# Graph attention stage on one core: four of a step's 14 incidence matrices built by VectorE in one op, and own-edge messages signalled tile by tile

## The chip, the cores and the metric

The kernel runs on one NeuronCore of a Trainium2 chip. Its engines are TensorE (PE, matrix products into PSUM), VectorE (DVE), ScalarE (ACT), GpSimd (POOL) and SyncE (SP, which issues transfers here). They run side by side and meet at semaphores: an instruction raises one when it is done, and another engine's queue stands until a semaphore has reached a number. Within an engine the instructions keep the order of the program. The metric is the device time of one execution, in microseconds (us).

## What is computed

The reference is a stack of four graph layers on 50000 nodes with 64 features and 50000 edges. Each layer normalises the nodes, passes messages along the edges and adds the result to its input. The change lies in the third, a graph attention layer with 4 heads, of which this is the part that matters:

```python
src = jnp.concatenate([src0, jnp.arange(n, dtype=src0.dtype)])
dst = jnp.concatenate([dst0, jnp.arange(n, dtype=dst0.dtype)])
...
amax = jax.ops.segment_max(alpha, dst, num_segments=n)
ex = jnp.exp(alpha - amax[dst])
denom = jax.ops.segment_sum(ex, dst, num_segments=n)
alpha = ex / (denom[dst] + SM_EPS)
out = jax.ops.segment_sum(x_l[src] * alpha[..., None], dst, num_segments=n)
out = out.mean(axis=1) + bias
```

Every node gets the sum of its incoming edges' messages, each weighted by a softmax over these edges, and one edge from itself (the `arange` part).

## The kernel before

The program is a sequence of stages, one block each with a barrier behind it: preparation, two graph layers (`norm_layer`), `edge_rows`, `segment_max`, `attention`, `batch_norm` and three typed layers. Only `attention` is touched. It walks over the nodes in 56 steps (`NS`) of 7 tiles (`HS`) of 128 nodes. The edges are sorted by destination, so the edges of a step lie in a window of 8 tiles (`WT`), and every node tile meets two tiles of edges (`BAND`): 14 pairs of tiles in a step.

A segment sum is a matrix product. For each pair a 128x128 incidence matrix (`S`, float32, 1 where an edge's destination is the node of the column) is made by comparing a row of node numbers with a column of the edges' destinations. In step n, by engine:

- GpSimd makes the 14 matrices of step n + 1, one instruction each (`matrices`, L2687), then splits the window's exponentials into three bfloat16 parts (`tails`, four small ops, L2696 to L2702), then makes the own-edge messages of tiles 4 to 6 of step n (`own_rest`, L2709).
- ScalarE makes the own-edge messages of tiles 0 to 3, four ops a tile (`own_edges`, L2633), casts the step's matrices to bfloat16 (`halves`, L2655), copies transposed sums out of PSUM (`turned`, L2642), takes the exponentials of small differences (`exps`, L2625) and writes an output (`outputs`, L2649).
- VectorE weights the window's messages of step n + 1 (`messages`, L2728), takes moments of a finished output (`moments`, L2755), then adds, per tile and head, the bank's sum times a weight to the own-edge message (`scale`, L2776, 28 ops), then works out the weights of step n + 1 (`differences` and `weights`, L2734 to L2749).
- TensorE forms the 14 weighted sums in four PSUM banks (`sums`, L2580), transposes those of the step before (`turns`, L2597), forms the sums of the exponentials (`small_sums`, L2569) and the output (`outputs`, L2604).

The matrices (`S`) and many other tiles exist twice, so that one step can be filled while the other is read. The own-edge messages (`mine`) exist once. The order on each engine is the order in which the code calls these functions; nothing is scheduled by a planner. The weights of a step are released by the semaphore `c_ok`, raised by L2749; it lets both makers of own-edge messages start. Ahead of its first op `scale` waits for all of them, by these lines, and then bank by bank for the sums:

```python
dve.wait_ge(mine_ok, n + 1)
dve.wait_ge(mine_p, n + 1)
```

In the profile the tiles of this stage are named `fa...` (`faS`, `famine`, `faagg`); `early` is a large buffer from which several tiles are cut (`M`, `own`, `small`, `d`, `cc`), and `alpha` lends its room to the window (`win`).

Of the kernel before, what the change touches and what calls it, by code (L numbers as in the profile page):

```python
# [4 lines left out]
P = 128  # L5
# [3 lines left out]
HS = 7  # L9
# [9 lines left out]
BAND = 2  # L19
# [10 lines left out]
def build_gnn(nc, a, out):  # L30
    f32, bf16, i32 = mybir.dt.float32, mybir.dt.bfloat16, mybir.dt.int32
    ALU, ACT, AX = mybir.AluOpType, mybir.ActivationFunctionType, mybir.AxisListType
# [45 lines left out]
    with ctx:  # L78
# [2405 lines left out]
        def attention(tag):  # L2484
            with nc.cleanup_on_exit(), ExitStack() as c, nc.Block() as block:
# [5 lines left out]
                ACT_TILES = 4  # L2491
                taken = [0]

                def carve(buf, shape):
                    n = 1
                    for k in shape[1:]:
# [8 lines left out]
                win = lent(alpha, 2 * WT * F, lambda shape: tb("win", shape))  # L2505
                S = tb("S", [P, 2, BAND * HS, P]); S_half = tb("S_half", [P, BAND * HS, P], bf16)
                PARTS = 3
                tail = tb("tail", [P, 2, WT, PARTS * E8], bf16); rest = tb("rest", [P, WT, E8])
                mine = tb("mine", [P, HS, HEADS, F]); agg = tb("agg", [P, 2, HS, HEADS, F])
                aggT = tb("aggT", [P, 2, HS * P]); oT = tb("oT", [2 * F, HS * P // 2])  # L2510
                stats = tb("stats", [2 * F, NS, 6]); mv = tb("mv", [F, 4])
                o_col2 = tb("o_col2", [2 * F, 1])
                win_in, ex_in, own_in = two("win_in"), two("ex_in"), two("own_in")
                (S_ok, M_ok, small_ok, small_read, d_ok, e_ok, c_ok, mine_ok, sums_ok, scaled, aT_made, aT_read, out_made, o_ok, stat_ok, stored, var_ok, sd_ok, half_ok, tail_ok, mine_p) = (
                    sm(n) for n in ("S_ok", "M_ok", "small_ok", "small_read", "d_ok", "e_ok", "c_ok", "mine_ok", "sums_ok", "scaled", "aT_made", "aT_read", "out_made",
                                    "o_ok", "stat_ok", "stored", "var_ok", "sd_ok", "half_ok", "tail_ok", "mine_p"))
                HALF = HS * P // 2
                both = S[0:F, 0, :, :].rearrange("p k c -> p (k c)")[:, 0:2 * NS * 6].rearrange("p (k c) -> p k c", c=6)
                CH = [(0, 4), (4, HS)]
# [99 lines left out]
                @block.scalar  # L2619
                def _(act):  # L2620
                    A = nc.scalar

                    def exps(n):
                        act.wait_ge(d_ok, n + 1)
                        A.activation(d[:, :, :, :], d[:, :, :, :], ACT.Exp).then_inc(e_ok, 1)  # L2625

                    def own_edges(n):
                        s = n % 2
                        act.wait_ge(c_ok, n + 1)
                        act.wait_ge(own_in[s], 16 * (n // 2 + 1))  # L2630
                        for t in range(ACT_TILES):
                            for h in range(HEADS):
                                ins = A.activation(mine[:, t, h, :], own[:, s, t, :], ACT.Copy, scale=cc[:, 1, t, h:h + 1])  # L2633
                        ins.then_inc(mine_ok, 1)

                    def turned(n):
                        for k, (b, q, to) in enumerate(TURNS):
                            t0, t1 = CH[b]
                            act.wait_ge(aT_made, 4 * n + k + 1)
                            if n >= 1 and k == 0:  # L2640
                                act.wait_ge(out_made, n)
                            A.copy(aggT[:, q, t0 * P:t1 * P], bank[to][:, 0:(t1 - t0) * P]).then_inc(aT_read, 1)  # L2642

                    def outputs(n):
                        if n >= 1:
                            act.wait_ge(stored, 32 * n)
                            act.wait_ge(stat_ok, n)
                        act.wait_ge(out_made, n + 1)
                        A.activation(oT[:, :], bank[5][:, 0:HALF], ACT.Identity, bias=o_col2[:, 0:1], scale=1.0 / HEADS).then_inc(o_ok, 1)  # L2649

                    def halves(n):
                        act.wait_ge(S_ok, n + 1)
                        if n >= 1:
                            act.wait_ge(small_ok, n)
                        A.copy(S_half[:, :, :], S[:, n % 2, :, :]).then_inc(half_ok, 1)  # L2655

                    halves(0)
                    for k in range(2):
                        ins = A.copy(o_col2[k * F:(k + 1) * F, :], o_col[:, :])
                    act.drain()  # L2660
                    exps(0)
                    for n in range(NS):
                        own_edges(n)
                        if n + 1 < NS:
                            halves(n + 1)
                        if n >= 1:
                            turned(n - 1)
                        if n + 1 < NS:
                            exps(n + 1)
                        if n >= 1:  # L2670
                            outputs(n - 1)
                    turned(NS - 1)
                    outputs(NS - 1)
                    act.wait_ge(var_ok, 1)
                    A.activation(mv[:, 2:3], mv[:, 1:2], ACT.Sqrt, bias=eps[0:F, 0:1]).then_inc(sd_ok, 1)

                @block.gpsimd
                def _(pool):
                    g = nc.gpsimd

                    def matrices(n):
                        s = n % 2
                        if n >= 2:
                            pool.wait_ge(sums_ok, NB * (n - 1))
                        for k in range(BAND * HS):
                            at = n * BAND * HS + k
                            ins = g.tensor_scalar(S[:, s, k, :], node_id[:, :], edge_id[:, at:at + 1], None, ALU.is_equal)  # L2687
                        ins.then_inc(S_ok, 1)

                    def tails(n):  # L2690
                        s = n % 2
                        pool.wait_ge(ex_in[s], 16 * (n // 2 + 1))
                        if n >= 2:
                            pool.wait_ge(small_ok, n - 1)
                        hi, mid, low = (tail[:, s, :, k * E8:(k + 1) * E8] for k in range(PARTS))
                        g.tensor_copy(hi, M[:, s, :, HF:MW])  # L2696
                        pool.drain()
                        g.tensor_tensor(rest[:, :, :], M[:, s, :, HF:MW], hi, ALU.subtract)
                        pool.drain()
                        g.tensor_copy(mid, rest[:, :, :])  # L2700
                        pool.drain()
                        g.tensor_tensor(low, rest[:, :, :], mid, ALU.subtract).then_inc(tail_ok, 1)  # L2702

                    def own_rest(n):
                        s = n % 2
                        pool.wait_ge(own_in[s], 16 * (n // 2 + 1))
                        pool.wait_ge(c_ok, n + 1)
                        k = HS - ACT_TILES
                        g.tensor_tensor(mine[:, ACT_TILES:HS, :, :], own[:, s, ACT_TILES:HS, :].unsqueeze(2).to_broadcast((P, k, HEADS, F)),  # L2709
                                        cc[:, 1, ACT_TILES:HS, :].unsqueeze(3).to_broadcast((P, k, HEADS, F)), ALU.mult).then_inc(mine_p, 1)  # L2710

                    matrices(0)
                    tails(0)
                    for n in range(NS):
                        if n + 1 < NS:
                            matrices(n + 1)
                            tails(n + 1)
                        own_rest(n)

                @block.vector  # L2720
                def _(dve):
                    v = nc.vector

                    def messages(n):
                        s = n % 2
# [37 lines left out]

                    def scale(n):
                        s = n % 2
                        dve.wait_ge(mine_ok, n + 1)
                        dve.wait_ge(mine_p, n + 1)
                        if n >= 2:
                            dve.wait_ge(aT_made, 4 * (n - 1))
                        v.drain()  # L2770
                        for b, (t0, t1) in enumerate(PAIRS):
                            dve.wait_ge(sums_ok, NB * n + b + 1)
                            for t in range(t0, t1):
                                for h in range(HEADS):
                                    lo = (t - t0) * HF + h * F
                                    ins = v.scalar_tensor_tensor(agg[:, s, t, h, :], bank[b][:, lo:lo + F], cc[:, 0, t, h:h + 1], mine[:, t, h, :], ALU.mult, ALU.add)  # L2776
                            ins.then_inc(scaled, 1)

                    v.tensor_tensor(amax[:, :, :], no_edge[:, :].unsqueeze(2).to_broadcast((P, T, HEADS)), amax[:, :, :], ALU.subtract)
                    messages(0)  # L2780
                    differences(0)
                    weights(0)
                    for n in range(NS):
                        if n + 1 < NS:
                            messages(n + 1)
                        if n >= 2:
                            moments(n - 2)
# [212 lines left out]
```

## Time and profile before

| | us |
|---|---|
| median of 3 timed runs (4918.04 to 4921.73) | 4918.32 |
| the profiled execution, its own time | 4923.76 |
| its span in the trace | 4922.2 |
| the attention stage, third `messages` op to the last | 696.02, 53 steps |

The profiled execution is 5.4 us above the median. All rows below are from it. Times in them are from the start of its span. Busy shares over the span mix stages with different limits; what sets the time of the attention stage is read from stretches inside it.

### The profile page before, as it was taken

To read this page: it belongs to the slowest core of one execution; us is meant where nothing else is said; L and a number is where in the kernel's file an instruction comes from. 1 tells how busy PE (TensorE), PEld (TensorE's weight loads), DVE (VectorE), ACT (ScalarE), POOL (GpSimd) and SP (SyncE) were. 2 spreads that over 40 slices of the span, in tenths; PEclk is the share of its full clock that TensorE was granted. 3 is DMA by queue.
4 is the path that set the end of the run, shared out by engine and by line. 5 is a ranking of instruction groups with operands and counts; after the bars stand their busy time and mean duration, and the time that the engine had idled before them with its cause. 6 is when DMAs were issued, how large, how long until landed. Compare 5 with 4: busy or idle time off the path is not lost. (4 is left out here: it accounts for less than half of the span.)

```text
span 4922.2 us, 87092 instructions
## 1 busy us (share of the span) xinstructions
PE 3747.6 (76%) x26626; PEld 3383.3 (69%) x26626; DVE 3240.1 (66%) x9139; ACT 2122.9 (43%) x5278; POOL 3217.5 (65%) x3814
## 2 busy tenths in 40 slices
PE   5720477748887999998388888795888688868888
PEld 5610467647887788887266666695888688868888
DVE  8978577757777777777577777784444344435544
ACT  6836244434444556555266565562222122212222
POOL 0011677747775777775499999546777577757775
PEclk9965687878888999999698999856989789888888
DMA  8013588757675666654222222265666466646664
GB/s 215 20 30 79 134 184 183 189 127 157 156 162 131 141 142 144 144 142 101 39 61 56 59 60 56 66 155 115 137 135 136 102 136 135 139 103 133 134 134 110
DMA packets 1661079, 588.72 MB, mean 120 GB/s; under 512 B 1564647, under 2 KB 1591078, under 8 KB 1660394
## 3 DMA queue, kind: packets, MB, share of 16 engines
q1 hardware_dynamic: 941766, 305.00, 27.3%
q10 hardware_dynamic: 636612, 195.74, 16.9%
q0 software_dynamic: 82272, 82.81, 8.6%
q8 instruction: 202, 3.31, 0.3%
q14 instruction: 227, 1.86, 0.1%
HBM read 387.27 MB, written 209.21 MB: 121 GB/s over the span
## 5 line engine op out<-in xcount | busy, mean ns | idle before, releaser
L2005 POOL DMA_INDIRECT early<-node_g,src_w x1173 | 1113.9, 950 | 425.1 <-issue 356.8
L2222 POOL DMA_INDIRECT early<-node_g,src_w x782 | 758.1, 969 | 296.0 <-issue 248.4
L2687 POOL TENSOR_SCALAR faS<-node_id,edge_id 128x128 f32<-128x128 f32 x784 | 464.5, 619 | 98.5 <-POOLq L1290 96.7
L1122 POOL DMA_INDIRECT fscat<-node_g,early x392 | 371.2, 947 | 164.6 <-issue 116.1
L1223 ACT ACTIVATE fslz<-bank 128x264 f32<-128x264 f32 x784 | 304.9, 392 | 201.2 <-PE bank L1174 151.5
L2266 PE MATMUL bank<-l0S,l0msg 128*128 128x128 f32 x1568 | 265.7, 347 | 163.3 <-issue 72.1
L2776 DVE SCALAR_TENSOR_TENSOR faagg<-bank,early,famine 128x64 f32<-128x64 f32 x1568 | 305.9, 274 | 123.9 <-POOL famine L2709 96.0
L2266 PEld LDWEIGHTS bank<-l0S,l0msg 128*128 128x128 f32 x1568 | 256.0, 259 | 170.2 <-issue 125.6
L2580 PEld LDWEIGHTS bank<-early,faS 128*128 128x128 f32 x1568 | 302.9, 196 | 100.6 <-issue 59.6
L2580 PE MATMUL bank<-early,faS 128*128 128x256 f32 x1568 | 366.3, 392 | 2.5 <-DVE faagg L2776 2.5
L1276 DVE TENSOR_TENSOR fslz<-fslz,bank 128x1848 f32<-128x1848 f32 x112 | 232.9, 2079 | 149.8 <-ACT fslz L1223 142.5
L2047 PE MATMUL bank<-l5S,l5msg 128*128 128x128 f32 x1568 | 230.7, 316 | 103.6 <-issue 68.7
L2047 PE MATMUL bank<-l3S,l3msg 128*128 128x128 f32 x1568 | 228.4, 314 | 104.7 <-issue 64.1
L2047 PE MATMUL bank<-l4S,l4msg 128*128 128x128 f32 x1568 | 233.7, 319 | 92.6 <-issue 59.2
L2047 PEld LDWEIGHTS bank<-l5S,l5msg 128*128 128x128 f32 x1568 | 222.1, 230 | 107.3 <-issue 107.3
L2047 PEld LDWEIGHTS bank<-l3S,l3msg 128*128 128x128 f32 x1568 | 219.6, 227 | 109.0 <-issue 108.8
L2047 PEld LDWEIGHTS bank<-l4S,l4msg 128*128 128x128 f32 x1568 | 225.1, 232 | 96.7 <-issue 96.6
L2263 PE MATMUL bank<-ident,l1own 128*64 128x128 f32 x784 | 184.9, 333 | 122.1 <-issue 72.3
L2266 PE MATMUL bank<-l1S,l1msg 128*64 128x128 f32 x1568 | 269.0, 300 | 0.0
L2147 DVE TENSOR_TENSOR l4msg<-early,bank 128x512 f32<-128x512 f32 x112 | 71.9, 683 | 275.0 <-DMA early<-edge_h 274.8
L2147 DVE TENSOR_TENSOR l3msg<-early,bank 128x512 f32<-128x512 f32 x112 | 71.9, 683 | 272.0 <-DMA early<-edge_h 271.9
L2633 ACT ACTIVATE famine<-early 128x64 f32<-128x64 f32 x896 | 220.1, 334 | 43.3 <-DVE early L2749 43.3
(400 smaller groups left out, 10433.4 us busy)
## 6 DMA issues: line engine op xcount, KB each, us to landing
edge_h<-early SPq DMA_DIRECT2D x280, 224.0 KB
node_g<-amax ACTq DMA_DIRECT2D x224, 224.0 KB
early<-edge_h SPq DMA_DIRECT2D x168, 256.0 KB
early<-node_g,src_w POOLq DMA_INDIRECT x1955
l0msg<-edge_a ACTq DMA_DIRECT2D x56, 256.0 KB
l0msg<-edge_h SPq DMA_DIRECT2D x56, 256.0 KB
l1msg<-edge_h SPq DMA_DIRECT2D x56, 256.0 KB
early<-dst_rows SPq DMA_DIRECT2D x56, 256.0 KB
```

The source lines that it names most:

```text
L1122: pool.indirect_dma_start(out=cat[:, s, t, lo:lo + F], out_offset=None, in_=node_g, in_offset=bass.IndirectOffsetOnAxis(ap=src_i[:, col], ...
L1223: A.activation(lz[:, kind, t, :], z_bank(g)[:, 0:ZW], ACT.Relu).then_inc(lz_ok, 1)
L1276: v.tensor_tensor(lz[:, kind, :, :], lz[:, kind, :, :], att_ps, ALU.mult)
L2005: pool.indirect_dma_start(out=ring[:, n % RING, t, :], out_offset=None, in_=table_in, in_offset=bass.IndirectOffsetOnAxis(ap=src_w[:, n * ...
L2047: nc.tensor.matmul(to, msg[:, s, t + q, :], S[:, s, BAND * t + q, :], start=(q == 0), stop=(q == BAND - 1))
L2222: pool.indirect_dma_start(out=ring[:, n % RING, t, :], out_offset=None, in_=table_in, in_offset=bass.IndirectOffsetOnAxis(ap=src_w[:, n * ...
L2263: nc.tensor.matmul(bank[2 * s + b][F:2 * F, col], own[:, d, t, :], ident[:, :], start=True, stop=True)
L2266: ins = nc.tensor.matmul(to, msg[:, d, t + q, :], S[:, s, BAND * t + q, :], start=(q == 0 and conv), stop=(q == BAND - 1))
L2580: ins = nc.tensor.matmul(bank[b][:, (t - t0) * HF:(t - t0 + 1) * HF], S[:, s, BAND * t + q, :], M[:, s, t + q, 0:HF], start=(q == 0), stop ...
L2633: ins = A.activation(mine[:, t, h, :], own[:, s, t, :], ACT.Copy, scale=cc[:, 1, t, h:h + 1])
L2687: ins = g.tensor_scalar(S[:, s, k, :], node_id[:, :], edge_id[:, at:at + 1], None, ALU.is_equal)
L2776: ins = v.scalar_tensor_tensor(agg[:, s, t, h, :], bank[b][:, lo:lo + F], cc[:, 0, t, h:h + 1], mine[:, t, h, :], ALU.mult, ALU.add)
```

## The change

VectorE makes the first four of a step's 14 matrices in one op (`first_matrices`), which compares the node numbers, repeated four times, with four columns of destinations; GpSimd makes the other ten. A new semaphore, `S_first`, tells ScalarE's cast that the four are there; GpSimd's `S_ok` tells of the ten. ScalarE raises `mine_ok` after each of its four tiles, not after the last alone. `scale` no longer waits ahead of its first op: it waits for `mine_ok` before each of the tiles 0 to 3, and for GpSimd's `mine_p` before tile 4.

```diff
+                WIDE_S = 4
...
                         for t in range(ACT_TILES):
                             for h in range(HEADS):
                                 ins = A.activation(mine[:, t, h, :], own[:, s, t, :], ACT.Copy, scale=cc[:, 1, t, h:h + 1])
-                        ins.then_inc(mine_ok, 1)
+                            ins.then_inc(mine_ok, 1)
...
                         act.wait_ge(S_ok, n + 1)
+                        act.wait_ge(S_first, n + 1)
...
-                        for k in range(BAND * HS):
+                        for k in range(WIDE_S, BAND * HS):
...
+                    def first_matrices(n):
+                        if n >= 2:
+                            dve.wait_ge(sums_ok, NB * (n - 1))
+                        at = n * BAND * HS
+                        v.tensor_tensor(S[:, n % 2, 0:WIDE_S, :], node_id[:, :].unsqueeze(1).to_broadcast((P, WIDE_S, P)),
+                                        edge_id[:, at:at + WIDE_S].unsqueeze(2).to_broadcast((P, WIDE_S, P)), ALU.is_equal).then_inc(S_first, 1)
...
-                        dve.wait_ge(mine_ok, n + 1)
-                        dve.wait_ge(mine_p, n + 1)
...
                             for t in range(t0, t1):
+                                if t < ACT_TILES:
+                                    dve.wait_ge(mine_ok, ACT_TILES * n + t + 1)
+                                elif t == ACT_TILES:
+                                    dve.wait_ge(mine_p, n + 1)
...
+                    first_matrices(0)
                     messages(0)
...
                         if n + 1 < NS:
+                            first_matrices(n + 1)
                             messages(n + 1)
```

On VectorE, a step from the release of the weights to the end of `scale` stands in the program before as

```order
L2749 TENSOR_TENSOR early<-early 128x56
L2728 TENSOR_TENSOR early<-alpha,early 128x8x256
L2755 BN_STATS fastats<-faoT 128x6
L2776 SCALAR_TENSOR_TENSOR faagg<-bank,early,famine 128x64 x28
L2734 TENSOR_REDUCE early<-bank 128x56
```

and on VectorE in the changed program, at the same place, as

```order
L2758 TENSOR_TENSOR early<-early 128x56
L2730 TENSOR_TENSOR faS<-node_id,edge_id 128x512
L2737 TENSOR_TENSOR early<-alpha,early 128x8x256
L2764 BN_STATS fastats<-faoT 128x6
L2787 SCALAR_TENSOR_TENSOR faagg<-bank,early,famine 128x64 x28
L2743 TENSOR_REDUCE early<-bank 128x56
```

The new op (L2730) stands between the op that releases the weights and `messages`; the rest keeps its order.

On GpSimd, a step of the loop in the program before is

```order
L2687 TENSOR_SCALAR faS<-node_id,edge_id 128x128 x14
L2696 CAST fatail<-early 128x8x8
L2698 TENSOR_TENSOR farest<-early,fatail 128x64
L2700 CAST fatail<-farest 128x8x8
L2702 TENSOR_TENSOR fatail<-farest,fatail 128x8x8
L2709 TENSOR_TENSOR famine<-early 128x768
```

and on GpSimd in the changed program

```order
L2689 TENSOR_SCALAR faS<-node_id,edge_id 128x128 x10
L2698 CAST fatail<-early 128x8x8
L2700 TENSOR_TENSOR farest<-early,fatail 128x64
L2702 CAST fatail<-farest 128x8x8
L2704 TENSOR_TENSOR fatail<-farest,fatail 128x8x8
L2711 TENSOR_TENSOR famine<-early 128x768
```

Four matrices are gone from each step, and nothing has changed places. TensorE and ScalarE issue the same instructions in the same order.

## Rows read from the trace of the kernel before

**Rows 1.** The page: busy us (share of the span) x instructions, by engine.
```profile
PE 3747.6 (76%) x26626; PEld 3383.3 (69%) x26626; DVE 3240.1 (66%) x9139; ACT 2122.9 (43%) x5278; POOL 3217.5 (65%) x3814
```

**Rows 2.** Busy time by stretch: third to last `messages` op.
```profile
core 0: us, PE busy (x) PEld busy (x) DVE busy (x) ACT busy (x) POOL busy (x), PEclk, DMA share, GB/s
2435.08:3131.10 696.02, 586.64 (x3391) 428.29 (x3390) 547.50 (x2014) 424.29 (x1219) 671.49 (x1007) 0.91 0.29 58
```

**Rows 3.** Who waited for whom, 2435 to 3131: total us, times, longest.
```profile
PE bank L2597 <- ACT faaggT L2642: 92.4, 48, 2.9
DVE faagg L2776 <- POOL famine L2709: 86.4, 41, 2.6
...
DVE faagg L2776 <- PE bank L2597: 18.3, 9, 2.0
...
PE bank L2604 <- ACT faaggT L2642: 16.7, 53, 0.3
DVE faagg L2776 <- PE bank L2580: 6.1, 3, 2.0
```

**Rows 4.** GpSimd's groups, 2435.08 to 3131.10: count | busy us, mean ns.
```profile
L2687 POOL TENSOR_SCALAR faS<-node_id,edge_id 128x128 f32<-128x128 f32 x742 | 434.4, 613 | 1.8 <-PE bank L2580 1.8
...
L2709 POOL TENSOR_TENSOR famine<-early 128x768 f32<-128x768 f32 x53 | 78.1, 1473 | 0.2
```

**Rows 5.** Instructions in order of time, one step: start us, us, what.
```profile
2815.90 0.22 DVE L2749 TENSOR_TENSOR early<-early 128x56 f32<-128x56 f32 x1
2816.03 2.28 DVE L2728 TENSOR_TENSOR early<-alpha,early 128x2048 f32<-128x2048 f32 x1
2816.15 3.93 ACT L2633 ACTIVATE famine<-early 128x64 f32<-128x64 f32 x16 [0.69 <-DVE early L2749]
...
2818.23 0.62 DVE L2755 BATCH_NORM_STATS2 fastats<-faoT 128x6 f32<-128x448 f32 x1
...
2819.26 1.48 POOL L2709 TENSOR_TENSOR famine<-early 128x768 f32<-128x768 f32 x1
...
2820.71 8.20 POOL L2687 TENSOR_SCALAR faS<-node_id,edge_id 128x128 f32<-128x128 f32 x14
2820.88 5.46 DVE L2776 SCALAR_TENSOR_TENSOR faagg<-bank,early,famine 128x64 f32<-128x64 f32 x28 [2.03 <-POOL famine L2709]
2821.56 1.80 ACT L2642 COPY faaggT<-bank 128x512 f32<-128x512 f32 x4
...
2826.26 0.32 DVE L2734 TENSOR_REDUCE early<-bank 128x56 f32<-128x168 f32 x1
...
2827.09 0.65 DVE L2739 TENSOR_SCALAR early<-early 128x28 f32<-128x28 f32 x1
```

**Rows 6.** VectorE's lines L2739 and L2728, all steps: duration ns min/median/max.
```profile
L2739 DVE TENSOR_SCALAR early<-early x56: 171/642/648, 2415.3 to 3142.1; 128x28 f32<-128x28 f32 x56
...
L2728 DVE TENSOR_TENSOR early<-alpha,early x56: 2278/2284/2345, 2404.7 to 3131.1; 128x2048 f32<-128x2048 f32 x56
```

**Rows 7.** The page's groups, a VectorE op of another stage: busy us, mean ns.
```profile
L2147 DVE TENSOR_TENSOR l4msg<-early,bank 128x512 f32<-128x512 f32 x112 | 71.9, 683 | 275.0 <-DMA early<-edge_h 274.8
```

**Rows 8.** Instructions in order of time, 2416.6 to 2419.8, GpSimd and VectorE.
```profile
2416.55 3.77 POOL L2687 TENSOR_SCALAR faS<-node_id,edge_id 128x128 f32<-128x128 f32 x3
...
2416.98 2.28 DVE L2728 TENSOR_TENSOR early<-alpha,early 128x2048 f32<-128x2048 f32 x1
```

**Rows 9.** Instructions in order of time, the stage's first steps.
```profile
2400.43 11.71 POOL L2687 TENSOR_SCALAR faS<-node_id,edge_id 128x128 f32<-128x128 f32 x14 [96.67 <-POOLq L1290]
...
2426.87 5.46 DVE L2776 SCALAR_TENSOR_TENSOR faagg<-bank,early,famine 128x64 f32<-128x64 f32 x28 [7.61 <-POOL famine L2709]
```

**Rows 10.** Instructions in order of time, the stage's last step.
```profile
3147.79 5.46 DVE L2776 SCALAR_TENSOR_TENSOR faagg<-bank,early,famine 128x64 f32<-128x64 f32 x28 [3.52 <-ACT famine L2633]
...
3153.31 0.88 PE L2597 MATMUL bank<-ident,faagg 128*128 128x128 f32 x6 [2.13 <-DVE faagg L2776]
```

**Rows 11.** Busy time by stretch: output matmuls of two steps; two earlier layers.
```profile
2810.20:2813.40 3.20, 3.20 (x9) 0.78 (x9) 3.20 (x17) 0.00 (x0) 3.20 (x6) 0.50 0.00 0
2836.50:2838.10 1.60, 1.60 (x8) 0.48 (x8) 1.60 (x10) 0.00 (x0) 1.60 (x4) 1.00 0.00 0
...
520.00:1030.00 510.00, 353.56 (x2287) 339.97 (x2288) 379.33 (x1156) 221.01 (x577) 374.51 (x387) 0.79 0.77 178
1070.00:1570.00 500.00, 400.38 (x3791) 385.71 (x3792) 362.02 (x1048) 222.24 (x576) 371.20 (x383) 0.87 0.70 154
```

More of the change, by code:

```diff
@@ L2513, in attention @@
                 win_in, ex_in, own_in = two("win_in"), two("ex_in"), two("own_in")
-                (S_ok, M_ok, small_ok, small_read, d_ok, e_ok, c_ok, mine_ok, sums_ok, scaled, aT_made, aT_read, out_made, o_ok, stat_ok, stored, var_ok, sd_ok, half_ok, tail_ok, mine_p) = (
+                (S_ok, M_ok, small_ok, small_read, d_ok, e_ok, c_ok, mine_ok, sums_ok, scaled, aT_made, aT_read, out_made, o_ok, stat_ok, stored, var_ok, sd_ok, half_ok, tail_ok, mine_p, S_first) = (
                     sm(n) for n in ("S_ok", "M_ok", "small_ok", "small_read", "d_ok", "e_ok", "c_ok", "mine_ok", "sums_ok", "scaled", "aT_made", "aT_read", "out_made",
-                                    "o_ok", "stat_ok", "stored", "var_ok", "sd_ok", "half_ok", "tail_ok", "mine_p"))
+                                    "o_ok", "stat_ok", "stored", "var_ok", "sd_ok", "half_ok", "tail_ok", "mine_p", "S_first"))
                 HALF = HS * P // 2
```

## The prediction

> **What bounds the kernel now.** The change touches one of the kernel's stages, attention, so I first cut the span down to it. The page's engine totals [rows 1] say little: TensorE 76%, GpSimd and VectorE some 65%, over stages with different limits. The stretch from the third `messages` op to the last holds 53 steps in 696.02 us, 13.13 us a step [rows 2]. Inside it GpSimd is busy 671.49 us, 96%, TensorE 84%, VectorE 79%, ScalarE 61%. GpSimd is full here and the others wait.
>
> Who waits for it is in the table of waits [rows 3]. VectorE's `scale` ops (L2776) wait for GpSimd's `mine` (L2709) in 41 steps, and for TensorE in 12. The 12 I count to GpSimd too: the table names whoever came last by the profile, and the waits are of the same 2.0 us or so. In the step laid out in [rows 5] `own_rest` ends at 2819.26 + 1.48 = 2820.74 and `scale` starts at 2820.88, 0.14 later. VectorE had been free since 2818.85, the end of its `bn_stats`. ScalarE's part of `mine` was ready at 2816.15 + 3.93 = 2820.08, and `scale` (28 ops in 5.46 us) takes the GpSimd part only from its 17th op on. So the loop is GpSimd's own row of work: 14 matrices, four small `tails` ops, `own_rest`; VectorE is dragged along by a wait placed ahead of all 28 ops.
>
> **The change part by part.**
>
> GpSimd loses four matrices a step. Their mean is 613 ns [rows 4], but they overlap a little: 14 take 8.20 us and the next op follows, 0.585 each, so 2.34 us a step. It gains a lock-out. While VectorE multiplies two SBUF operands, GpSimd stands: in [rows 8] three matrices, 1.8 us by themselves, take 3.77 us beside `messages`, 2.0 us more for an op of 2.28. The new op is a quarter as long; I charge 0.5 (bounds 0 and 0.68, its whole length). GpSimd then needs 13.13 - 2.34 + 0.5 = 11.3 us a step.
>
> VectorE gains one op, 512 elements a partition, two SBUF operands, float32. The nearest row is a 128x512 tensor_tensor at 683 ns [rows 7]; `messages`, four times as wide, takes 2284 [rows 6]. Consecutive VectorE ops overlap by 0.08 (2816.03 to 2818.23 for an op of 2.28 [rows 5]), so 0.60 us a step. Bounds: 0.53 (a quarter of 2.28 less overlap) and 0.68.
>
> VectorE loses its wait. Over the 53 steps it is 86.4 + 18.3 + 6.1 = 110.8 us, 2.09 a step [rows 3]. Not all of it goes: behind `bn_stats` stand two drains and the waits, and I keep 0.28 for them, twice the 0.14 that the row shows from the release to the first op. So 1.81 us go. The last 12 `scale` ops still need `own_rest`, but from its start `scale` has 16 x 0.19 = 3.1 us of work before that, and GpSimd with 11.3 us a step has time to spare. The waits that now stand between tiles cost nothing that I can see: the 28 ops already contain three such waits (one for each later bank) and run at 0.19 each without a gap.
>
> VectorE's step is then 13.13 - 1.81 + 0.60 = 11.92 us. One term in it depends on the phase against GpSimd. L2739, a tiny op, takes 171 ns at the least and 642 in the median [rows 6]; it is held by GpSimd's matrix in flight. In the new order VectorE comes to it some 9.9 us after the weights are released (0.60 + 2.20 + 0.62 + 0.28 + 5.38 + 0.83 us from the new op to L2739 [rows 5]); GpSimd by then has stood out the lock, made `own_rest` and is at its last matrix or in the shorter `tails` ops. Between no stall (11.45) and the usual one (11.92) I take 11.8, nearer to the row.
>
> This holds only if TensorE and ScalarE keep up. TensorE is busy 586.64/53 = 11.07 us a step [rows 2] and cannot avoid the 16.7/53 = 0.31 ahead of its output matmuls [rows 3]; its wait for ScalarE (92.4 us, 1.74 a step) shrinks when the step does. 11.4 us: under 11.8, with little room. ScalarE has its `mine` ops, the cast and the copies behind each other: begun at 2816.15, they are through at 2821.56 + 1.80 = 2823.36 [rows 5], 7.2 us later and well inside a step. It waits now also for the new op, which is done 0.7 us after the release, while the cast comes 3.9 us after it: nothing. Loads are issued about a step ahead of use, as now.
>
> On the lock itself the rows and a rule part. In [rows 8] GpSimd's matrices run from 2416.55 without a break; VectorE's `messages` starts at 2416.98, inside one, and still takes its 2.28, as it does in all 56 steps (2278 to 2345 ns [rows 6]). GpSimd pays, VectorE does not. The Trainium skill, SBUF — State Buffer, section Who interferes with whom, says that a VectorE op with two SBUF inputs and a GpSimd op that reads SBUF exclude each other, and that whichever issues first keeps the port for its whole length. By that rule VectorE would sometimes wait for GpSimd, and its sum would be that of the third rival below. The trace agrees for the single-input L2739, which waits, and not for the two-input `messages`; I go by the row of the same kind.
>
> The first two steps gain by themselves [rows 9]. GpSimd's first 14 matrices take 11.71 us; four fewer and one lock more bring the next work 1.85 us forward, and the second set as much again: `own_rest` of step 0 ends 3.7 us earlier. `scale` of step 0 waited 7.61 us for it; now 16 of its 28 ops run before, 3.1 us. Less the new op, 6.2 us.
>
> In the last step `scale` waited 3.52 us for all of ScalarE's tiles and TensorE's last transposes 2.13 us for `scale` [rows 10]. Tile by tile, that 2.13 goes; I book 2.1.
>
> **Sum:** 6.2 + 53 x (13.13 - 11.8) + 2.1 = 6.2 + 70.5 + 2.1 = 78.8 us. The profiled execution took 4923.76 us, so 4845.0; it lies 5.4 above the median of the timed runs, 4918.32, which becomes 4839.5. I say 4840.
>
> **The rivals.**
>
> *TensorE sets the pace.* With 11.07 us busy in a step of 11.8 it would be 94% busy. Its granted clock in the stage is 0.91 on average [rows 2], but between the two levels: the eight output matmuls fill 3.2 us at 0.50 (1.2 GHz) in one step and 1.6 at 1.00 (2.4 GHz) in another [rows 11]; before both the engine had waited for ScalarE. In the first two graph layers, with 69 and 80% busy, the granted clock is 0.79 and 0.87 [rows 11]. At the mean of these, 0.83, TensorE needs 11.07 x 0.91/0.83 + 0.31 = 12.45 us a step: a gain of 53 x 0.68 + 8.3 = 44.3 us, 4874. For it: TensorE has no slack to speak of. Against: the waits that precede the slow stretches get shorter, and a slow step is caught up in the next as long as the queue of finished sums holds. Chance 0.17.
>
> *The wait only changes its name.* `scale` now starts on time but is held at its 17th op, because GpSimd's lock-out costs what the four matrices saved. That needs a lock of 2.34 us from an op of 0.68; or the waits for TensorE in [rows 3] are real. Then the start and end terms remain, 8.3 us: 4910. Chance 0.04.
>
> *VectorE waits for GpSimd* (slower). The release of the weights frees GpSimd's `own_rest` at the very moment when VectorE's new op begins. If `own_rest` (1473 ns [rows 4]) gets the port first, the new op waits 1.47 us, and `messages` behind it, with the port changing hands between the two, waits another matrix of 0.58: 11.92 + 2.05 = 13.97 us a step, 53 x 0.84 - 8.3 = 36 us more, 4954. It decides from about 1.35 us of such waiting a step. For it: L2739 does wait. Against: `messages` never did, and it starts 0.13 us after the start of the op that releases the weights [rows 5], before the release can reach GpSimd. The rule quoted above from the Trainium skill speaks for this case. Chance 0.05.
>
> *Better than forecast:* L2739 meets no matrix and the small costs vanish: 11.45, 53 x 1.68 + 8.3 = 97.3 us, 4821. That is the low end of the forecast's own range; beyond it 0.04.
>
> **How the numbers follow.** The forecast, a VectorE-bound step of 11.45 to 12.1 us (4821 to 4855), has 0.70. The range of 8 in 10 takes in its low end with a little room and the TensorE rival: 4815 to 4876. Left out are the renamed wait, the slower case and the tail below, 0.13, and some of TensorE's. A measurement of this kernel tells about 0.2%, 10 us, from no change. Faster than that are the forecast, the better case and the TensorE rival: 0.91. Same, the renamed wait: 0.04. Slower: 0.05.
>
> **What would show it.** Right: steps of 11.8 us, GpSimd's busy share of the stage falling from 96% to some 92% of a shorter step (12.67 - 2.34 + 0.5 of 11.8 us), its idle time before `own_rest`, waiting for the weights; the wait of `scale` for `mine` gone; the new op at about 0.68; `messages` at 2.28 still. Wrong in the lock: the new op or `messages` longer than these, or starting late. Wrong in TensorE: waits of `scale` for bank sums, and output matmuls at 0.50 in most steps. Wrong in the phase: L2739 always at 0.64, or a new stall at its neighbours. Other stages should keep their times within a few us; if they move, my sum is not about the change.

## The result and the profile after

The change makes the kernel 0.5% faster: 4896.34 us median of 6 runs against 4918.18 of 6, ratio 0.9947, 95% interval 0.9937 to 0.9957. That is 22 us where 79 were forecast, and above the 4876 at which the stated range ends. The span of the profiled execution falls from 4922.2 to 4894.1 us.

The stage after, by stretch as in [rows 2], from the third `messages` op to the last (the same 53 steps):

```profile
core 0: us, PE busy (x) PEld busy (x) DVE busy (x) ACT busy (x) POOL busy (x), PEclk, DMA share, GB/s
2429.96:3105.80 675.84, 572.26 (x3382) 424.85 (x3381) 620.80 (x2067) 424.39 (x1220) 503.76 (x801) 0.93 0.30 60
```

675.84/53 = 12.75 us a step, against 13.13 before and 11.8 in the forecast. The 20.2 us saved in these steps, 5.1 ahead of them (2435.08 to 2429.96) and what is left behind them make up the 28.1 us of the span. GpSimd is no longer full: 75%. VectorE is now the fullest, 92% busy, and by the waits below it stands for others only in small pieces (16.7 us in all for ScalarE's `exps`, 0.3 at a time). Who waited for whom, 2430 to 3106 (us in total, times, longest), where [rows 3] stood before:

```profile
ACT early L2626 <- DVE early L2748: 212.0, 53, 4.4
...
PE bank L2598 <- ACT faaggT L2643: 86.8, 49, 4.5
POOL famine L2711 <- DVE early L2758: 79.3, 50, 2.1
POOL faS L2689 <- PE bank L2581: 69.6, 49, 3.3
...
DVE early L2752 <- ACT early L2626: 16.7, 53, 0.3
```

The waits of `scale`, 110.8 us before, 86.4 of them put down to GpSimd's `mine`, are gone but for some 15 us in short pieces, as forecast. GpSimd waits instead, for the weights ahead of `own_rest` and for TensorE's sums ahead of its matrices. So VectorE's own ops must have grown. Three of its and GpSimd's lines over all steps (duration ns min/median/max):

```profile
L2730 DVE TENSOR_TENSOR faS<-node_id,edge_id x56: 677/684/724, 2403.4 to 3105.2; 128x512 f32<-128x512 f32 x56
...
L2737 DVE TENSOR_TENSOR early<-alpha,early x56: 2282/3560/3561, 2406.8 to 3105.8; 128x2048 f32<-128x2048 f32 x56
...
L2711 POOL TENSOR_TENSOR famine<-early x56: 1472/1787/3517, 2422.8 to 3118.1; 128x768 f32<-128x768 f32 x56
```

The new op costs what was forecast, 0.68 us. `messages`, which never took more than 2.35 us [rows 6], now takes 3.56: 1.28 us more, in 50 of the 56 steps. One step in order of time shows what stands in its way:

```profile
2809.74 0.22 DVE L2758 TENSOR_TENSOR early<-early 128x56 f32<-128x56 f32 x1
2809.88 0.68 DVE L2730 TENSOR_TENSOR faS<-node_id,edge_id 128x512 f32<-128x512 f32 x1
2809.99 3.93 ACT L2634 ACTIVATE famine<-early 128x64 f32<-128x64 f32 x16 [0.69 <-DVE early L2758]
2810.10 1.79 POOL L2711 TENSOR_TENSOR famine<-early 128x768 f32<-128x768 f32 x1 [1.35 <-DVE early L2758]
2810.48 3.56 DVE L2737 TENSOR_TENSOR early<-alpha,early 128x2048 f32<-128x2048 f32 x1
```

L2758 ends at 2809.96 and releases the weights. GpSimd, which has waited 1.35 us for them, starts `own_rest` at 2810.10, beside the new op. `messages` starts at 2810.48, before `own_rest` has ended (2811.89), and ends 2.15 us behind that end: its own length, less the 0.13 us by which its start may overlap. Early in the stage, while GpSimd is still in its `tails` ops when the weights come, it goes otherwise:

```profile
2452.29 0.22 DVE L2758 TENSOR_TENSOR early<-early 128x56 f32<-128x56 f32 x1
2452.42 0.68 DVE L2730 TENSOR_TENSOR faS<-node_id,edge_id 128x512 f32<-128x512 f32 x1
...
2453.02 2.32 DVE L2737 TENSOR_TENSOR early<-alpha,early 128x2048 f32<-128x2048 f32 x1
2453.35 2.16 POOL L2700 TENSOR_TENSOR farest<-early,fatail 128x64 f32<-128x64 f32 x1
...
2456.29 1.47 POOL L2711 TENSOR_TENSOR famine<-early 128x768 f32<-128x768 f32 x1
```

Here it is GpSimd's op that stands (2.16 us for one of 0.31), `own_rest` comes after, and the steps up to the next two releases take 12.0 and 11.85 us. From the step at 2476 on GpSimd has caught up and waits at the release, and the long `messages` is there for good.

### The profile page after: what moved, and what is told of

Read it like the earlier page. It is cut to its first block and busy times, and to the rows that moved or that the text cites. A ratio compares the mean times of both kernels' runs of the same rounds, so it can differ in the third digit from the quotient of the medians.

```text
span 4894.1 us, 87037 instructions
## 1 busy us (share of the span) xinstructions
PE 3752.4 (77%) x26626; PEld 3401.5 (70%) x26626; DVE 3316.4 (68%) x9195; ACT 2123.6 (43%) x5278; POOL 3043.4 (62%) x3590
## 5 line engine op out<-in xcount | busy, mean ns | idle before, releaser
L2689 POOL TENSOR_SCALAR faS<-node_id,edge_id 128x128 f32<-128x128 f32 x560 | 373.8, 690 | 164.4 <-POOLq L1290 94.8
L2266 PE MATMUL bank<-l0S,l0msg 128*128 128x128 f32 x1568 | 279.1, 360 | 159.0 <-issue 83.5
L2266 PEld LDWEIGHTS bank<-l0S,l0msg 128*128 128x128 f32 x1568 | 269.6, 271 | 165.4 <-issue 142.0
L1174 PE MATMUL bank<-Wea,fseaT 65*128 65x264 f32 x784 | 238.5, 385 | 0.0
```

Source lines behind the costliest of these rows:

```text
L1174: nc.tensor.matmul(z_bank(g)[:, 0:ZW], eaT[:, s, t * P:(t + 1) * P], Xea[0:F + 1, :], start=False, stop=True).then_inc(z_ok, 1)
L2266: ins = nc.tensor.matmul(to, msg[:, d, t + q, :], S[:, s, BAND * t + q, :], start=(q == 0 and conv), stop=(q == BAND - 1))
```

## The experiments

Theory A: `own_rest`, set free while the new op runs, gets its operands read between the new op and `messages`, and `messages` stands for it. Rival B: `messages` is slow because a wide op with two SBUF operands stands directly ahead of it. Rival C: another engine would hold the step anyway. Steps in the table are the mean of 52 steps, from the release of step 2 to that of step 54; "ratio" is to the kernel before on the same chip, where a kernel was timed more than once.

| kernel | us | ratio, 95% | step | `messages`, median |
|---|---|---|---|---|
| before | 4918.18 | | 13.13 | 2.28 |
| changed | 4896.34 | 0.9947 (0.9937 to 0.9957) | 12.78 | 3.56 |
| own_behind_messages | 4849.63 | 0.9857 (0.9841 to 0.9874) | 11.91 | 2.28 |
| new_op_alone | 4904.32 | 0.9968 (0.9956 to 0.9981) | 12.82 | 3.56 |
| tile_waits_alone | 4912.66 | 0.9983 (0.9973 to 0.9992) | 13.01 | 2.28 |
| new_op_two_ahead | 4834.44 | 0.9823 (0.9807 to 0.9840) | 11.63 | 2.28 |
| new_op_behind_messages | 4897.60 | 0.9955 (0.9938 to 0.9971) | 12.79 | 2.29 |
| own_rest_two_tiles | 4873.87 | one run | 12.46 | 3.13 |
| own_rest_four_tiles | 4918.65 | one run | 13.25 | 3.99 |
| own_rest_in_three | 4853.46 | one run | 12.09 | 2.70 |
| matrix_behind_release | 4834.94 | 0.9828 (0.9812 to 0.9845) | 11.69 | 2.28 |
| own_rest_small_first | 4857.06 | one run | 11.97 | 2.48 |
| two_ahead_two_wide | 4843.01 | one run | 11.88 | 2.28 |
| two_ahead_six_wide | 4847.53 | one run | 11.91 | 2.28 |

**Take the meeting away.** One wait more on GpSimd, in `own_rest`:

```diff
                         pool.wait_ge(c_ok, n + 1)
+                        if n + 1 < NS:
+                            pool.wait_ge(M_ok, n + 2)
```

> The changed kernel, with one wait more on GpSimd: own_rest of step n also waits for M_ok of messages of step n + 1. Theory A (own_rest, released while the new op runs, gets its operands read between the new op and messages, and messages stands until it is done): messages back from 3.56 to 2.28 us in all steps, own_rest starts some 2.9 us after the weights' release, steps of 11.4 to 12.0 us, 4832 to 4856 us. Rival B (messages is slow because another wide op of two SBUF operands stands directly ahead of it on VectorE, whoever else runs): messages stays at 3.56, 4890 to 4900 us. Rival C (TensorE or ScalarE would hold the step at its length anyway): messages at 2.28, but scale then waits for bank sums or own edges, 4880 us or more.

A step in order of time:

```profile
2808.20 0.68 DVE L2732 TENSOR_TENSOR faS<-node_id,edge_id 128x512 f32<-128x512 f32 x1
...
2808.81 2.28 DVE L2739 TENSOR_TENSOR early<-alpha,early 128x2048 f32<-128x2048 f32 x1
2811.01 0.61 DVE L2766 BATCH_NORM_STATS2 fastats<-faoT 128x6 f32<-128x448 f32 x1
2811.26 1.47 POOL L2713 TENSOR_TENSOR famine<-early 128x768 f32<-128x768 f32 x1 [3.04 <-DVE early L2739]
```

The new op still stands directly ahead of `messages`, and that takes 2.28 us again: B falls. A wait in which GpSimd stands for 3.04 us in this step takes some 45 us off the time of the changed kernel, so C falls too. The step is 11.91 us, beside the 11.92 of the forecast's sum with L2739's usual stall.

**The parts of the change apart.** In the first, the two old waits stand again ahead of `scale` and the tile waits are gone; in the second, `WIDE_S = 0`, without `first_matrices` and without ScalarE's wait for it.

> The changed kernel with the old waits ahead of scale: all own-edge messages before its first op. Theory A: in the steady steps both makers are done before scale can start (own_rest 1.93 us after the release, ScalarE's four tiles 3.9 us after it, scale starts at 4.9), so the tile-by-tile waits are worth nothing there: steps of 12.83, messages 3.56; only the first two and the last step lose, 4896 to 4905 us. Rival (the finer waits carry the gain that there is): 4910 us or more.

> The changed kernel without the new op: GpSimd makes all 14 matrices, the tile-by-tile waits stay. GpSimd's row of work is unchanged, 13.1 us a step, so theory A and my sum both say 4912 to 4918 us, the last step's 2 to 3 us and some of the first steps' apart; scale waits at its 17th op for own_rest instead of ahead of its first. Rival (the early start of scale shifts VectorE against GpSimd so that messages meets own_rest here too): messages over 2.4 us and 4920 us or more.

Both as theory A had them. With the new op alone the steady steps are nearly as long as with both parts (12.82 against 12.78 us), because `own_rest` now ends 1.9 us after the release and ScalarE's tiles 3.9 us after it, before `scale` can begin at 4.9. The tile waits are worth 9.1 us between the two profiled spans: 6.0 ahead of the release of step 2, 2.1 over the 52 steps, 1.0 behind them. With the tile waits alone GpSimd's 14 matrices keep the step at 13.0 us, and `scale` waits in its middle:

```profile
2801.48 3.16 DVE L2786 SCALAR_TENSOR_TENSOR faagg<-bank,early,famine 128x64 f32<-128x64 f32 x16 [0.29 <-ACT famine L2634]
2804.98 1.48 POOL L2710 TENSOR_TENSOR famine<-early 128x768 f32<-128x768 f32 x1
2806.56 2.39 DVE L2786 SCALAR_TENSOR_TENSOR faagg<-bank,early,famine 128x64 f32<-128x64 f32 x12 [1.92 <-POOL famine L2710]
```

**The new op in other places.** Two steps ahead, behind `scale`:

```diff
                     first_matrices(0)
+                    first_matrices(1)
...
                         if n + 1 < NS:
-                            first_matrices(n + 1)
                             messages(n + 1)
...
                         scale(n)
+                        if n + 2 < NS:
+                            first_matrices(n + 2)
```

> The changed kernel with the new op moved: VectorE makes the four matrices of step n + 2 behind scale of step n, not ahead of messages. Theory A: the release of the weights is followed at once by messages, as in the kernel before, so messages holds the port first: 2.28 us, own_rest behind it; the new op now meets GpSimd's matrices, of which one (0.6 us) may stand in its way: 0.68 to 1.3 us. Steps of 11.5 to 12.3 us, 4835 to 4875 us. Rival B: messages at 2.28 too, and the op behind the new one slow instead. Rival C: 4880 us or more.

and in the changed kernel's place with the two calls exchanged:

> The changed kernel with messages and the new op exchanged on VectorE. Theory A: messages holds the port first and is back at 2.28 us; own_rest, waiting since the release, steps in between messages and the new op, and now it is the new op that stands: some 1.95 us for 0.68. The step stays at 12.6 to 12.9 us, 4880 to 4900 us. Rival D (own_rest would not get in behind so long an op, or the loss hangs on messages alone): the new op at 0.68, steps of 11.5 to 12.0, 4832 to 4856 us.

Two ahead, `messages` follows the release at once and is under way before the release can set `own_rest` going, and the step is 11.63 us. The new op, amid GpSimd's matrices, loses at most 0.14 us (0.68 in the median, 0.82 at the most). The time, 4834 us, lies just below the 4835 to 4875 that were expected. Exchanged, the loss moves to whichever VectorE op comes second, with the same 1.28 us:

```profile
L2730 DVE TENSOR_TENSOR faS<-node_id,edge_id x56: 683/1962/1967, 2407.6 to 3111.8; 128x512 f32<-128x512 f32 x56
...
L2737 DVE TENSOR_TENSOR early<-alpha,early x56: 2283/2286/2334, 2410.6 to 3109.6; 128x2048 f32<-128x2048 f32 x56
```

**The dose.** The length of `own_rest` is changed by `ACT_TILES = 5` and `ACT_TILES = 3`, and then cut into three ops of one tile each.

> The changed kernel with the own edges shared 5 tiles to ScalarE and 2 to GpSimd: own_rest of 512 elements, some 1.0 us. Theory A: messages at 3.56 - 0.48 = 3.1 us; steps of 12.35 us, 4865 to 4880 us. Rivals B and C: messages unchanged at 3.56.

> The changed kernel with the own edges shared 3 tiles to ScalarE and 4 to GpSimd: own_rest of 1024 elements, some 1.95 us. Theory A: the wait of messages grows with it, 3.56 + 0.48 = 4.0 us; steps of 13.3 us, 4915 to 4930 us. Rivals B and C: messages unchanged at 3.56.

> The changed kernel with own_rest made by three ops of one tile each, not by one of three tiles. Theory A, with the port handed over at each instruction's end: messages waits for the first of the three alone, 2.28 + 0.3 to 0.5 = 2.6 to 2.8 us, the other two come behind it; steps of 11.9 to 12.2 us, 4845 to 4870 us. Rival (VectorE waits until GpSimd has nothing more to read): messages waits for all three, 3.6 us or more.

`messages` with two and with four tiles in `own_rest`, and with the first of three ops in its way:

```profile
L2737 DVE TENSOR_TENSOR early<-alpha,early x56: 2279/3132/3136, 2404.3 to 3086.4; 128x2048 f32<-128x2048 f32 x56
```
```profile
L2737 DVE TENSOR_TENSOR early<-alpha,early x56: 2279/3992/3996, 2408.4 to 3133.7; 128x2048 f32<-128x2048 f32 x56
```
```profile
L2738 DVE TENSOR_TENSOR early<-alpha,early x56: 2284/2701/2706, 2403.1 to 3066.9; 128x2048 f32<-128x2048 f32 x56
```

Over 2.28 us that is 0.42 us for an op of 256 elements in the way, 0.85 for 512, 1.28 for 768, 1.71 for 1024: a line through zero, 1.67 ns an element. Cut in three, `messages` stands for the first of the three ops alone.

**What lets a matrix pass.** The row that misled the forecast had matrices beside `messages`. Here the last of GpSimd's ten matrices is put where `own_rest` was: behind the wait for the weights, ahead of `own_rest` (lines of the edit that bear on the order).

```diff
                         pool.wait_ge(c_ok, n + 1)
+                        if n + 1 < NS:
+                            last_matrix(n + 1)
```

> The changed kernel with one of GpSimd's ten matrices (0.6 us, 128 elements) put behind the wait for the weights, ahead of own_rest, so that a matrix and not own_rest is what the release sets free. Theory E (GpSimd keeps messages out for the time of its op's elements, 1.67 ns each by the runs with two, three and four tiles, not for the op's length): the matrix keeps messages out for 0.2 us at most, own_rest comes 0.6 us after it and finds messages at work: messages 2.28 to 2.5, own_rest stretched to 3.5, steps of 11.7 to 12.1 us, 4840 to 4860 us. Rival F (it is out for the op's length less the new op's end): messages 2.28 + 0.6 - 0.2 = 2.7 us and steps of 12.1 to 12.4, 4860 to 4880 us. Rival G (own_rest still gets in first): 3.5 us or more.

Better than either theory had it; one step in order of time:

```profile
2804.23 0.68 DVE L2738 TENSOR_TENSOR faS<-node_id,edge_id 128x512 f32<-128x512 f32 x1
...
2804.49 3.03 POOL L2696 TENSOR_SCALAR faS<-node_id,edge_id 128x128 f32<-128x128 f32 x1 [0.45 <-DVE early L2766]
2804.83 2.28 DVE L2745 TENSOR_TENSOR early<-alpha,early 128x2048 f32<-128x2048 f32 x1
```

The matrix starts 0.34 us before `messages`, and still it is the matrix that stands, 3.03 us for 0.6, while `messages` loses nothing. Theory E had it the other way round, the matrix through first and `own_rest` stretched, so E was wrong, and issue order alone does not decide. Size or kind? The last run cut `own_rest` into ops of 128, 128 and 512 elements, the first as small as a matrix.

> The changed kernel with own_rest made by three ops of 128, 128 and 512 elements. A matrix of 128 elements, set free at the same moment, cost messages nothing, own-edge ops of 256 to 1024 cost it 1.67 ns an element. If it is the size of the op that lets messages pass, the first small op costs nothing either and messages stays at 2.28. If it is the kind of op (a tensor_tensor of two SBUF operands asks for the port at once, a tensor_scalar later), the line holds down to 128 elements: messages at 2.28 + 0.21 = 2.49 us. Steps of 11.7 to 12.2 us, 4835 to 4860 us either way.

```profile
L2743 DVE TENSOR_TENSOR early<-alpha,early x56: 2283/2481/2491, 2405.9 to 3064.2; 128x2048 f32<-128x2048 f32 x56
```

`messages` takes 2.48 us: the line holds down to 128 elements (0.2 us), so at this place it is the kind of op that counts and not its size. Why the tensor_scalar comes too late is open. It is not free at every place: in tile_waits_alone a matrix is in flight at all 56 starts of `messages`, which takes 2.28 us in the median, but up to 2.46 where the matrix began only just before it.

**The share.** Two other widths in new_op_two_ahead, each timed once.

> new_op_two_ahead with two matrices on VectorE and twelve on GpSimd. By the sum GpSimd needs 13.13 - 1.17 + 0.2 = 12.2 us a step and is the bound again, VectorE some 0.27 less than with four: steps of 12.0 to 12.3 us, 4855 to 4870 us. If VectorE bounds alone: 4815 to 4825 us.

> new_op_two_ahead with six matrices on VectorE and eight on GpSimd. By the sum VectorE is the bound and gains 256 elements, 0.27 us a step: 11.6 + 0.27 = 11.9 us, 4845 to 4855 us. If GpSimd or TensorE bounds: the same time as with four or less, 4835 us or under.

With two, GpSimd is the bound again (482 of 500 us busy), but at 11.88 us, 0.3 less than I had: my price for GpSimd's step was too high by that. With six, VectorE pays for 256 elements more as forecast (0.95 us for the new op, 11.91 a step). By the step, four is the best of the three.

## Why the prediction was wrong, point by point

- **The bound before** was read rightly: the wait of `scale` was for GpSimd, and it went. GpSimd's share of the stage was forecast at 92% and came to 75%. The 12.67 us busy a step from which the forecast started held some 2.0 us in which the `tails` op L2698 stood beside `messages`; in the changed kernel that op (L2700) meets `messages` in one step alone:

```profile
L2698 POOL TENSOR_TENSOR farest<-early,fatail x56: 307/2330/2337, 2412.5 to 3131.2; 128x64 f32<-128x64 f32 x56
```
```profile
L2700 POOL TENSOR_TENSOR farest<-early,fatail x56: 307/308/2162, 2411.9 to 3103.9; 128x64 f32<-128x64 f32 x56
```

- **Prices of the parts.** The new op 0.68 us (683 ns was the row taken), GpSimd relieved, the start 5.1 us for 6.2, the last step and what follows 2.8 for 2.1: right or near. The sum for VectorE's step, 11.92 us with L2739's usual stall, comes close to the 11.91 of own_behind_messages. The mean lengths of L2738 and L2739 add up to 0.76 us before and 0.74 there; in matrix_behind_release they add up to 0.47, and the step is 11.69. The forecast's 11.8 lies between. One slip had no effect: the lower bound of the new op, a quarter of 2.28 less the overlap, is 0.49 and not 0.53.
- **The step that failed** is the one on the lock: "GpSimd pays, VectorE does not ... I go by the row of the same kind." The row [rows 8] had GpSimd's matrices beside `messages`; the op that the change sets free at that moment is `own_rest`, another kind, which no row showed against `messages`, since in the kernel before it came after it (2819.26 against 2816.03 [rows 5]). The forecast put VectorE's loss to GpSimd at nothing, and `messages` lost 1.28 us a step. Over 50 steps that is 64 us, less about 0.3 us a step by which L2739 and its neighbours came out shorter than forecast: some 50 us, and by the profiled executions the gain was 28.1 us, 50.7 short of the 78.8. The "never" of [rows 6] was also a matter of order: in 48 of the 56 steps before, the op beside `messages` was L2698, a tensor_tensor of GpSimd like `own_rest`, which began some 0.1 us after `messages` and stood for it, and in the other 8 it was a matrix. In the changed kernel the new op stands in the place behind the release, and `messages` comes second.
- **The third rival** had the right mechanism one op too early and too large: it had `own_rest` go ahead of the new op, and VectorE lose 2.05 us in two waits; the new op came first and the loss was one wait of 1.28, of `messages`. By the forecast's own sum some 1.35 us would have decided the sign, so it came close. It had a chance of 0.05; that `own_rest` now waits for its release, which the same text forecast, should have raised it. The sentence against it, that the new op starts before the release can reach GpSimd, was true and did not help: `own_rest` slipped in behind the new op.
- What the Trainium skill states in SBUF — State Buffer, section Who interferes with whom, that two-input VectorE ops and GpSimd ops that read SBUF exclude each other and the later one waits, agrees with `own_rest` against `messages` (3.56 for 2.28 us). It does not agree with matrix_behind_release, where the op that started 0.34 us earlier is the one that waits, and there the measurement decides. L2739, which the forecast counted for the rule as quoted, has one SBUF input and so does not bear on it.
- **TensorE as the bound** fell. In the stretch 2500 to 3000 its busy time rose from 423.84 us of 500 before to 446.35 in new_op_two_ahead, whose step of 11.63 us is shorter than the forecast's, and the granted clock with it, from 0.90 to 0.97, where 1.00 is 2.4 GHz and 0.50 is 1.2 GHz (columns as in the first row above; before, then new_op_two_ahead):

```profile
2500.00:3000.00 500.00, 423.84 (x2429) 307.60 (x2428) 393.60 (x1447) 304.25 (x875) 482.05 (x725) 0.90 0.29 58
```
```profile
2500.00:3000.00 500.00, 446.35 (x2754) 338.15 (x2753) 455.53 (x1678) 345.31 (x989) 454.39 (x642) 0.97 0.33 66
```

## What to carry to other kernels

When work moves from GpSimd to VectorE, ask which GpSimd op will stand waiting at a release, and what VectorE issues right behind that release: where two VectorE ops with two SBUF operands stood in a row here, a tensor_tensor of GpSimd that was set free during the first went ahead of the second, and the second stood for it. Let the longest such op follow the release at once, or hold GpSimd's op back until it is done; here these gave some 60 and 45 us more than the change's own 22. A row that shows two engines meeting without loss speaks only for the two kinds of op that met, and for the order in which they came.

## What was not expected of the hardware

A tensor_tensor of GpSimd that is set free while VectorE's first op runs keeps the second out for 1.67 ns an element from 128 to 1024 elements, 0.19 us less than its length where it has 768 (1.28 of 1.47 us). A tensor_scalar of GpSimd, started 0.34 us before VectorE's op at the same place, keeps it out not at all and stands itself (3.03 us for 0.6). TensorE's clock was granted more, not less, in the kernel in which TensorE was busier (0.97 at 89% busy, 0.90 at 85%).
